# Mixer's context keys: the low word of each first key half made on VectorE from PSUM

## The chip, the cores and the metric

One core of one Trainium2 chip runs the whole program in one launch. The metric is the device time of one execution in microseconds; several runs are taken and their median is compared. One further execution is profiled.

## The reference

The program is a two-layer latent network on x (4 x 256 x 256) and a context (4 x 4096 x 256), all in float32. Each step is added to x and works on a layer-normed x:

```python
x = x + L0_xattn(_layernorm(x), ctx, ctx, mask, ...)    # 1 head of width 1024, masked
x = x + L0_attn(_layernorm(x), ...)                     # the mixer: a selective scan
x = x + L0_ffn(_layernorm(x), ...)                      # soft mixture of experts
x = x + L1_xattn(_layernorm(x), ctx, ctx, ...)          # 16 heads of width 16
x = x + L1_attn(_layernorm(x), ...)                     # causal attention
x = x + L1_ffn(_layernorm(x), ...)                      # quantised MLP
```

The change touches the second line, in which the kernel also prepares the fourth. The mixer is, cut short:

```python
xx, res = split(x @ in_w.T);  xx = silu(causal_conv4(xx) + conv_b)
delta, B, C = split(xx @ xproj_w.T);  delta = softplus(delta @ dt_w.T + dt_b)
state = exp(delta * A) * state + delta * B * xx      # over 256 tokens, 512 channels, 16 states
y = (sum over states of C * state + xx * D) * silu(res);  out = y @ out_w.T
```

and the part of the fourth line that does not depend on x is k = key @ Wk.T + bk and v = value @ Wv.T + bv, for all 4 x 4096 rows of the context.

## The kernel before

All six steps run one after the other, with a barrier of all engines behind each (`mixer` ends with one). The stage in question is `mixer`. While its scan runs, a second stream of work, called the context, computes k and v of the fourth step and stores them to DRAM. Products of the context are exact to about float32 by words: an operand is held as a high word, rounded to the format that TensorE multiplies in one pass, and a low word, the remainder; `products` (line 149) multiplies high by high, high by low and low by high.

**The mixer's scan.** 64 units: 2 halves of the tokens x 4 tiles of 128 channels (m) x 8 pairs of states (q); `mx_unit` gives them. For a unit i ScalarE makes two decays into PSUM (`prepare`, line 1115, instruction at 1123), GpSimd multiplies delta * u by B (`inputs`, 911, at 923), VectorE scans (`recur`, 1204, at 1208), multiplies by C (`outputs`, 1217), adds the two states of every second unit (`added`, 1222), and TensorE sums into a PSUM bank by a product with the identity (`total`, 987, at 998). Decays of unit i wait for the scan of unit i - 2. In the first tile of channels of each half (units 0 to 7 and 32 to 39) TensorE also spreads rows of B and C over all partitions (`spread`, 977, at 984) and ScalarE copies them out (1113). Every eight units come ScalarE's steps of softplus: Abs and Exp (`decline`, 1093 and 1095) in units 1, 9, 17 and so on, Ln with table loads (`logarithm`, 1099) in units 4, 12, 20 and so on, with VectorE's parts at 1178, 1180, 1186, 1188 and 1198, and VectorE's gate at 1230 and 1233.

**The context.** 32 chunks of 512 context rows, four steps each (`Steps`, line 614): first key half (128 of 256 output channels), second key half, first values, second values. A key half m of chunk i goes so. TensorE makes six products into one PSUM bank (`keys`, 677). ScalarE reads the bank, adds bk and writes the high word (`rounded` with n = 0, line 728). TensorE then adds to the same bank the product of the negated identity and that high word (`remainder`, 685, product at 687), so that the bank holds the difference. ScalarE reads it again with bk added and writes the low word (`rounded` with n = 1, same line). SyncE stores both (`store_keys`, 638, at 641). A values step is 12 products of 256 columns (`values`, 690) and two copies by ScalarE (738). SyncE fetches the next chunks (635).

**The order** is written out by hand. Every engine goes through its own list of units, and `mx_context(new, part)` (803) says how many context steps are done by the first place (part 0, ahead of the unit's decays on ScalarE and of its sums on TensorE) and by the second (part 1, behind them). Units 0 to 7 and 32 to 39 take one step each, in the second place; the others take two or three. The first step of a chunk i stands in these units: chunks 1, 2, 17, 18 in 0, 4, 32, 36 (second place), in which `CTX_ALONE` (581) puts the remainder right behind the keys; chunks 3, 5, 6, 9, 10, 12, 13, 16 in 8, 11, 13, 18, 20, 23, 25, 30, and 19, 23, 24, 25, 29, 30, 31 in 40, 47, 49, 51, 58, 60, 62 (first place); chunks 4, 7, 8, 11, 14, 15 in 9, 14, 16, 21, 26, 28, and 20, 21, 22, 26, 27, 28 in 41, 43, 45, 52, 54, 56 (second place). Chunk 0 is done ahead of the scan. On ScalarE and TensorE a step of one half is interleaved with the remainder of the other, as the `step` functions show.

**The banks.** Three PSUM banks (5, 6, 7) are handed round in the order of `MX_ORDER` among keys, values, step sizes and spreads; `free` (934) makes TensorE wait until the user three places earlier is through with the bank, and for keys that is when the semaphore kr of that half has reached 2n + 2 (`mx_taken`, 855):

```python
def mx_taken(s, cs, kind, n, part=0):
    if kind == "keys":
        return cs[2][part], 2 * n + 2
```

In units 8 to 31 and 40 to 63, where no spreads are made, second values of a chunk so follow its first key half in the same bank.

Of the kernel before, what the change touches and what calls it, by code (L numbers as in the profile page):

```python
# [6 lines left out]
F32 = mybir.dt.float32  # L7
# [665 lines left out]
def context_pe(k, t, sems, bank, free):  # L673
    s, kp, kr, ks = sems
    pe, PS = k.pe, k.PS

    def keys(i, m):
        if i == 0:
            pe.wait_ge(s.words, 5)
        free("keys", i, m)  # L680
        wait_chunk(pe, s, i)
        products(k, PS[:, bank("keys", i, m), :], [[t["wk2"][:, a, kd, m * P:(m + 1) * P] for a in range(2)] for kd in range(KD)],
                 [[t["words"][:, i % 2, a, kd, :] for a in range(2)] for kd in range(KD)]).then_inc(kp[m], 1)

    def remainder(i, m):
        pe.wait_ge(kr[m], 2 * i + 1)
        pe.matmul(PS[:, bank("keys", i, m), :], t["minus"][:], t["keys"][:, m, 0, :], start=False, stop=True,
                  skip_group_check=True).then_inc(kp[m], 1)

    def values(i, pair):  # L690
        free("values", i, pair)
        for j in range(2):
            at = (2 * pair + j) * P
            last = products(k, PS[:, bank("values", i, pair), j * D:(j + 1) * D],
                            [[t["words"][:, i % 2, a, kd, at:at + P] for a in range(2)] for kd in range(KD)],
                            [[t["wv2"][:, a, kd, :] for a in range(2)] for kd in range(KD)])
        last.then_inc(s.vp, 1)

    def step(n):
        i, sub = n // 4, n % 4  # L700
        if i in CTX_ALONE and sub < 2:
            keys(i, sub)
            remainder(i, sub)
        elif i in CTX_ALONE:
            values(i, sub - 2)
        elif sub == 0:
            keys(i, 0)
        elif sub == 1:
            keys(i, 1)
            remainder(i, 0)  # L710
        elif sub == 2:
            values(i, 0)
            remainder(i, 1)
        else:
            values(i, 1)

    return Steps(step)


def context_act(k, t, sems, bank):  # L720
# [1 line left out]
    act = k.act  # L722

    def rounded(i, m, n):
        act.wait_ge(kp[m], 2 * i + n + 1)
        if n == 0 and i:
            act.wait_ge(ks[m], 32 * i)
        act.activation(t["keys"][:, m, n, :], k.PS[:, bank("keys", i, m), :], ACT.Identity,  # L728
                       bias=t["bk"][:, m:m + 1]).then_inc(kr[m], 1)
# [12 lines left out]
    def step(n):  # L742
        i, sub = n // 4, n % 4
        if i in CTX_ALONE and sub < 2:
            rounded(i, sub, 0)
            rounded(i, sub, 1)
        elif i in CTX_ALONE:
            values(i, sub - 2)
        elif sub == 0:
            rounded(i, 0, 0)  # L750
        elif sub == 1:
            rounded(i, 1, 0)
            rounded(i, 0, 1)
        elif sub == 2:
            values(i, 0)
            rounded(i, 1, 1)
        else:
            values(i, 1)

    return Steps(step)  # L760

# [382 lines left out]

def mixer_dve(k, t, s, ct, cs):
    dve, PS, DT = k.dve, k.PS, MX_DT
    norm_dve(k, 1)
    yt_dve(k, 1)

    dve.wait_ge(s.small, 80)  # L1150
    for m in range(DT):
# [4 lines left out]
        for j in range(1, MX_TAPS):  # L1156
            dve.wait_ge(s.tap, MX_TAPS * m + j)
            dve.scalar_tensor_tensor(u, t["xpad"][:, m % 2, :, j:j + S], t["conv_w"][:, m, j:j + 1], u,
                                     ALU.mult, ALU.add).then_inc(s.tap, 1)

    for half in range(2):
        b, cols = mx_bank(16 + half), slice(half * BANK, (half + 1) * BANK)
# [72 lines left out]
    for i in range(MX_UNITS + MX_SUM):  # L1235
        if i < MX_UNITS:
            recur(i)
        if mx_chunk(i, 7):
            remainder(mx_chunk(i, 7))
        if mx_chunk(i, 4):  # L1240
# [5 lines left out]
            outputs(i - MX_MUL)  # L1246
        if 0 <= i - MX_ADD < MX_UNITS and mx_added(i - MX_ADD):
            added(i - MX_ADD)
    for tile in range(NT):
        dve.wait_ge(s.out, tile + 1)  # L1250
        dve.tensor_tensor(k.X[:, tile, :], k.X[:, tile, :], PS[:, tile % 2, 0:D], ALU.add).then_inc(s.x, 1)
# [1737 lines left out]
```

## Time and profile before

| | |
|---|---|
| median of 3 runs | 2008.87 us (2008.55 to 2012.26) |
| the profiled execution's own time | 2010.82 us |
| its span, first to last instruction | 2009.5 us |
| mean granted clock of TensorE | 0.945 |
| first keys of the context at | 355.2 us |
| first and last scan start at | 404.9 and 742.6 us |

The profiled execution's time is its span and what lies around it. In the tables of rows, times are microseconds from the span's start, unless marked ns. PE is TensorE, PEld its weight loads, DVE VectorE, ACT ScalarE, POOL GpSimd, SPq the queue of SyncE. A row of a group by line has line, engine and operation, output <- inputs with shapes, count, then busy us and mean ns of one, then the idle time of the engine just before them and what ended it. A row of the timeline has start, length, engine, line, operation and shapes; xN says that N such followed each other, and the bracket gives the idle time before. Matmuls overlap, so that the distance from one's start to the next one's is shorter than a matmul's own length.

### The profile page before, as it was taken

What the parts mean: (1) busy time and instruction counts of PE and PEld (TensorE: products, weight loads), DVE (VectorE), ACT (ScalarE), POOL (GpSimd) and SP (SyncE); (2) the same over time, 40 slices, a digit from 0 to 9 for tenths busy, and PEclk for the clock granted to TensorE, in tenths of its full rate; (3) what the DMA queues carried; (4) which work ended last, traced back from release to release, by engine and by line L of the source; (5) the groups of instructions that cost most, each with busy time, mean ns of one, the idle gap of its engine ahead of it and who ended that gap; (6) DMA issues with size and microseconds to landing.
All of it is one profiled execution on the core that took longest, in us unless ns stands there. A gap on an engine that the chain in (4) does not pass through costs nothing. (4 is left out here: it accounts for less than half of the span.)

```text
span 2009.5 us, 32823 instructions
## 1 busy us (share of the span) xinstructions
PE 1791.3 (89%) x12553; PEld 1223.2 (61%) x12553; DVE 1469.5 (73%) x1717; ACT 1202.4 (60%) x2131; POOL 368.3 (18%) x238
## 2 busy tenths in 40 slices
PE   7989998879988994999997899999999999998754
PEld 5877776447755663788877455555555555555524
DVE  7646552468888884566664699999999999994475
ACT  1332332577777753344443288888888888993363
POOL 4223301035444441122222000010010000000000
PEclk8999998989999997999999799999999999998977
DMA  9798852128855862121214945566657646510000
GB/s 360 275 322 313 314 198 90 53 79 307 283 211 192 289 242 87 49 90 64 70 38 74 164 120 117 102 112 119 119 109 123 115 103 112 102 28 10 0 1 21
DMA packets 171769, 280.20 MB, mean 139 GB/s; under 512 B 21422, under 2 KB 100430, under 8 KB 164446
## 3 DMA queue, kind: packets, MB, share of 16 engines
q1 hardware_dynamic: 169886, 277.61, 49.0%
q8 instruction: 102, 1.67, 0.4%
q10 hardware_dynamic: 1728, 0.49, 0.1%
q14 instruction: 53, 0.43, 0.1%
HBM read 187.46 MB, written 88.14 MB: 137 GB/s over the span
## 5 line engine op out<-in xcount | busy, mean ns | idle before, releaser
L2321 DVE TENSOR_REDUCE xn_peaks<-psum 128x2 f32<-128x1024 f32 x512 | 621.9, 1224 | 40.3 <-PE psum L2128 32.4
L2278 ACT ACTIVATE moe_mix_transposed<-psum 128x512 f32<-128x512 f32 x1024 | 552.8, 597 | 70.4 <-PE psum L2133 20.9
L2133 PE MATMUL psum<-xn_q_stack,xn_k_words 50*128 50x256 f32 x2048 | 376.2, 306 | 6.7 <-DVE xn_peaks L2321 4.7
L2128 PE MATMUL psum<-xn_k_words,xn_q_stack 50*128 50x512 f32 x1024 | 372.2, 452 | 5.6 <-DMA xn_q_stack<-q_rows 4.0
L2133 PEld LDWEIGHTS psum<-xn_q_stack,xn_k_words 50*128 50x128 f32 x2048 | 249.3, 186 | 208.1 <-ACT moe_mix_transposed L2278 186.8
L2165 PE MATMUL psum<-moe_mix_transposed,xn_v 128*32 128x256 f32 x4096 | 328.2, 392 | 2.0 <-issue 0.3
L923 POOL TENSOR_TENSOR mx_state<-mx_du,mx_b_all_channels 128x1024 f32<-128x1024 f32 x64 | 156.4, 2444 | 237.1 <-ACT mx_c_all_channels L1113 114.5
L2128 PEld LDWEIGHTS psum<-xn_k_words,xn_q_stack 50*128 50x128 f32 x1024 | 185.7, 186 | 14.9 <-issue 9.1
L1208 DVE TENSOR_TENSOR_SCAN mx_state<-psum,mx_state 128x1024 f32<-128x1024 f32 x64 | 146.2, 2284 | 57.9 <-ACT psum L1123 37.8
L321 PE MATMUL psum<-xw_ctx_natural,xw_weights_transposed 128*128 128x256 f32 x512 | 126.7, 394 | 14.0 <-DVE xw_weights_transposed L473 13.7
L2165 PEld LDWEIGHTS psum<-moe_mix_transposed,xn_v 128*32 128x32 f32 x4096 | 81.7, 108 | 73.6 <-issue 8.0
L728 ACT ACTIVATE ctx_k_words<-psum,ctx_bk 128x512 fp32r<-128x512 f32 x128 | 85.3, 688 | 50.8 <-PE psum L153 41.1
L153 PE MATMUL psum<-ctx_chunk_words,ctx_wk_words 128*128 128x512 f32 x384 | 109.3, 427 | 7.0 <-DMA ctx_chunk_words<-ctx_words 4.0
L153 PE MATMUL psum<-ctx_wv_words,ctx_chunk_words 128*128 128x256 f32 x768 | 115.1, 300 | 0.1
L321 PEld LDWEIGHTS psum<-xw_ctx_natural,xw_weights_transposed 128*128 128x128 f32 x512 | 96.4, 197 | 29.2 <-DVE xw_weights_transposed L473 17.1
L153 PEld LDWEIGHTS psum<-ctx_wv_words,ctx_chunk_words 128*128 128x128 f32 x768 | 101.4, 192 | 17.1 <-issue 13.2
L1974 POOL CAST xn_neg_words<-xn_neg_max 128x4 fp32r<-128x4 f32 x32 | 6.1, 190 | 549.2 <-DVE xn_neg_max L2328 549.2
L153 PE MATMUL psum<-moe_w_words,moe_hidden_words 128*128 128x256 f32 x768 | 101.8, 291 | 5.2 <-issue 5.2
L153 PE MATMUL psum<-xw_ctx_transposed_words,xw_q_folded_words 128*128 128x512 f32 x384 | 100.2, 417 | 3.6 <-DVE xw_scores L455 3.0
L153 PE MATMUL psum<-moe_slot_input_words,moe_w_words 128*128 128x512 f32 x384 | 93.8, 400 | 10.2 <-ACT moe_hidden L1548 8.6
L153 PEld LDWEIGHTS psum<-moe_w_words,moe_hidden_words 128*128 128x128 f32 x768 | 95.9, 192 | 8.9 <-issue 8.9
L998 PE MATMUL psum<-mx_state,identity 128*128 128x512 f32 x192 | 96.2, 619 | 2.5 <-DVE mx_state L1222 2.5
(330 smaller groups left out, 2647.2 us busy)
## 6 DMA issues: line engine op xcount, KB each, us to landing
xn_k_words<-k_words SPq DMA_DIRECT2D x384, 128.0 KB, 6.4
ctx_words<-xw_ctx_transposed_words SPq DMA_DIRECT2D x64, 512.0 KB, 7.1
ctx_chunk_words<-ctx_words SPq DMA_DIRECT2D x64, 512.0 KB, 5.4
k_words<-ctx_k_words SPq DMA_DIRECT2D x128, 256.0 KB, 2.5
v_all<-ctx_v SPq DMA_DIRECT2D x32, 544.0 KB, 3.2
xn_v<-v_all SPq DMA_DIRECT2D x32, 544.0 KB, 5.0
xw_mask<-in_mask_BxSxS_ik SPq DMA_DIRECT2D x8, 2048.0 KB, 7.9
xw_ctx_natural<-in_ctx SPq DMA_DIRECT2D x32, 512.0 KB, 6.6
```

Of the source, the lines that this page charges most:

```text
L153: last = k.pe.matmul(out, l, r, start=(n == 0), stop=(n == len(terms) - 1))
L321: last = pe.matmul(PS[:, 5, 0:D], t["ET"][:, c % 2, j, :], t["ctxN"][:, c, j, :], start=(c + j == 0), stop=(c == CH - 1 and j == JC - 1))
L728: act.activation(t["keys"][:, m, n, :], k.PS[:, bank("keys", i, m), :], ACT.Identity, bias=t["bk"][:, m:m + 1]).then_inc(kr[m], 1)
L923: pool.tensor_tensor(t["state"][:, i % MX_STATES, :, :], t["du"][:, m % 2, None, :].to_broadcast([P, MX_NQ, MX_HALF]), t["Bb"][:, q * MX_N ...
L998: last = pe.matmul(PS[:, MX_Y, :], k.ident[:], t["state"][:, i % MX_STATES, j, :], start=(q + j == 0), stop=(q == MX_NU - 1 and j == parts ...
L1208: dve.tensor_tensor_scan(flat, t["decay"][i % MX_DECAYS].rearrange("p n t -> p (n t)"), flat, 0.0, ALU.mult, ALU.add).then_inc(s.scan, 1)
L1974: pool.tensor_copy(t["neg_words"][:, :, :, XN_SHIFT], neg).then_inc(s.words, 1)
L2128: return pe.matmul(PS[:, 2 * (x % 2) + a, :], Q[narrow_rows(a), m // XN_PAIRS % 2, m % XN_PAIRS, q * P:(q + 1) * P], K[m % XN_KSLOTS][narr ...
L2133: return pe.matmul(PS[:, narrow_bank("exp", n, step, a), half * S:(half + 1) * S], K[n % XN_KSLOTS][narrow_rows(a), kt * P:(kt + 1) * P], ...
L2165: last = pe.matmul(PS[W * j:W * (j + 1), XN_ACC, 0:S], t["V"][:, n % 2, at:at + W], t["weights"][:, step % 4, a, half, :], start=(step == ...
L2278: act.activation(t["weights"][:, step % 4, a, :, :], bank.rearrange("p (t s) -> p t s", t=2), ACT.Exp, scale=XN_SCALE).then_inc(s.taken, 1)
L2321: dve.tensor_reduce(t["peaks"][:, m % 2, q, :, c], PS[:, 2 * (x % 2):2 * (x % 2) + 2, :], AX.X, ALU.max).then_inc(s.top_read, 1)
```

## The change

For the first key half (m = 0) of every chunk, TensorE's product with the negated identity and ScalarE's second rounding go. In their place VectorE reads the bank once: (bank + bk) - high word, written as the low word, one scalar_tensor_tensor of 128x512 per chunk. The second key half stays as it was. ScalarE's rounding of a first half now waits for kp[0] at i + 1, since TensorE increments it once per chunk. VectorE waits for that rounding (kr[0] at 2i + 1) and itself brings kr[0] to 2i + 2, for which the stores and the next user of the bank wait, as before. VectorE's context steps stand behind its convolution (chunk 0) and else behind the scan of each unit, up to the steps of both places of that unit.

```diff
--- before.py
+++ after.py
@@ -700,14 +700,14 @@
         i, sub = n // 4, n % 4
         if i in CTX_ALONE and sub < 2:
             keys(i, sub)
-            remainder(i, sub)
+            if sub:
+                remainder(i, sub)
         elif i in CTX_ALONE:
             values(i, sub - 2)
         elif sub == 0:
             keys(i, 0)
         elif sub == 1:
             keys(i, 1)
-            remainder(i, 0)
         elif sub == 2:
             values(i, 0)
             remainder(i, 1)
@@ -722,7 +722,7 @@
     act = k.act
 
     def rounded(i, m, n):
-        act.wait_ge(kp[m], 2 * i + n + 1)
+        act.wait_ge(kp[m], 2 * i + n + 1 if m else i + 1)
         if n == 0 and i:
             act.wait_ge(ks[m], 32 * i)
         act.activation(t["keys"][:, m, n, :], k.PS[:, bank("keys", i, m), :], ACT.Identity,
@@ -743,19 +743,37 @@
         i, sub = n // 4, n % 4
         if i in CTX_ALONE and sub < 2:
             rounded(i, sub, 0)
-            rounded(i, sub, 1)
+            if sub:
+                rounded(i, sub, 1)
         elif i in CTX_ALONE:
             values(i, sub - 2)
         elif sub == 0:
             rounded(i, 0, 0)
         elif sub == 1:
             rounded(i, 1, 0)
-            rounded(i, 0, 1)
         elif sub == 2:
             values(i, 0)
             rounded(i, 1, 1)
         else:
             values(i, 1)
+
+    return Steps(step)
+
+
+
+
+def context_dve(k, t, sems, bank):
+    s, kp, kr, ks = sems
+    dve = k.dve
+
+    def step(n):
+        i, sub = n // 4, n % 4
+        if sub == 0:
+            dve.wait_ge(kr[0], 2 * i + 1)
+            if i:
+                dve.wait_ge(ks[0], 32 * i)
+            dve.scalar_tensor_tensor(t["keys"][:, 0, 1, :], k.PS[:, bank("keys", i, 0), :], t["bk"][:, 0:1],
+                                     t["keys"][:, 0, 0, :].bitcast(F32), ALU.add, ALU.subtract).then_inc(kr[0], 1)
 
     return Steps(step)
 
@@ -1144,6 +1162,7 @@
 
 def mixer_dve(k, t, s, ct, cs):
     dve, PS, DT = k.dve, k.PS, MX_DT
+    ctx = context_dve(k, ct, cs, mx_bank_of)
     norm_dve(k, 1)
     yt_dve(k, 1)
 
@@ -1157,6 +1176,7 @@
             dve.wait_ge(s.tap, MX_TAPS * m + j)
             dve.scalar_tensor_tensor(u, t["xpad"][:, m % 2, :, j:j + S], t["conv_w"][:, m, j:j + 1], u,
                                      ALU.mult, ALU.add).then_inc(s.tap, 1)
+    ctx.upto(MX_EARLY)
 
     for half in range(2):
         b, cols = mx_bank(16 + half), slice(half * BANK, (half + 1) * BANK)
@@ -1235,6 +1255,7 @@
     for i in range(MX_UNITS + MX_SUM):
         if i < MX_UNITS:
             recur(i)
+            ctx.upto(mx_context(i, 1))
         if mx_chunk(i, 7):
             remainder(mx_chunk(i, 7))
         if mx_chunk(i, 4):
@@ -1246,6 +1267,7 @@
             outputs(i - MX_MUL)
         if 0 <= i - MX_ADD < MX_UNITS and mx_added(i - MX_ADD):
             added(i - MX_ADD)
+    ctx.upto(CTX_STEPS)
     for tile in range(NT):
         dve.wait_ge(s.out, tile + 1)
         dve.tensor_tensor(k.X[:, tile, :], k.X[:, tile, :], PS[:, tile % 2, 0:D], ALU.add).then_inc(s.x, 1)
```

## Rows read from the trace of the kernel before

**Rows 1.** The page: busy time, share of the span and instructions of each engine.

```profile
PE 1791.3 (89%) x12553; PEld 1223.2 (61%) x12553; DVE 1469.5 (73%) x1717; ACT 1202.4 (60%) x2131; POOL 368.3 (18%) x238
```

**Rows 2.** Windows of the mixer: length, busy per engine, granted clock, DMA share, GB/s.

```profile
456.48:584.43 127.95, 118.85 (x591) 89.18 (x590) 106.42 (x82) 95.30 (x177) 57.69 (x24) 0.99 0.82 291
632.24:745.00 112.76, 107.22 (x543) 80.95 (x541) 100.02 (x76) 83.71 (x157) 54.84 (x23) 1.00 0.80 288
```

**Rows 3.** Groups by line, units 0 to 63; columns as in the page.

```profile
L1208 DVE TENSOR_TENSOR_SCAN mx_state<-psum,mx_state 128x1024 f32<-128x1024 f32 x64 | 146.2, 2284 | 57.9 <-ACT psum L1123 37.8 <-POOL mx_state L923 20.1
L728 ACT ACTIVATE ctx_k_words<-psum,ctx_bk 128x512 fp32r<-128x512 f32 x124 | 82.6, 688 | 49.2 <-PE psum L153 39.6 <-PE psum L687 5.3 <-DMA k_words<-ctx_k_words 4.3
L687 PE MATMUL psum<-ctx_k_words,ctx_minus_identity 128*128 128x512 f32 x62 | 26.6, 430 | 22.9 <-ACT ctx_k_words L728 22.7
L1230 DVE SCALAR_TENSOR_TENSOR mx_u<-mx_u,mx_skip,psum 128x512 f32<-128x512 f32 x7 | 5.0, 719 | 0.0
```

**Rows 4.** Timeline around chunk 19: start, us, engine, line, idle before and its end.

```profile
632.22 0.40 PE L687 MATMUL psum<-ctx_k_words,ctx_minus_identity 128*128 128x512 f32 x1
632.24 2.28 DVE L1208 TENSOR_TENSOR_SCAN mx_state<-psum,mx_state 128x1024 f32<-128x1024 f32 x1
632.45 1.60 PE L153 MATMUL psum<-ctx_wv_words,ctx_chunk_words 128*128 128x256 f32 x12
...
634.09 0.65 ACT L738 COPY ctx_v<-psum 128x256 f32<-128x256 f32 x2 [0.43 <-PE psum L153]
634.44 1.51 DVE L1217 TENSOR_TENSOR mx_state<-mx_state,mx_c_all_channels 128x1024 f32<-128x1024 f32 x1
...
635.84 1.28 ACT L1123 ACTIVATE psum<-mx_delta,mx_a 128x510 f32<-128x510 f32 x2
...
637.15 2.29 DVE L1208 TENSOR_TENSOR_SCAN mx_state<-psum,mx_state 128x1024 f32<-128x1024 f32 x1 [1.21 <-ACT psum L1123]
```

**Rows 5.** Timeline: scans 13, 14, 20, 21, 51 and 52, and a copy of values.

```profile
483.54 2.28 DVE L1208 TENSOR_TENSOR_SCAN mx_state<-psum,mx_state 128x1024 f32<-128x1024 f32 x1
...
487.72 2.27 DVE L1208 TENSOR_TENSOR_SCAN mx_state<-psum,mx_state 128x1024 f32<-128x1024 f32 x1
...
519.77 2.29 DVE L1208 TENSOR_TENSOR_SCAN mx_state<-psum,mx_state 128x1024 f32<-128x1024 f32 x1 [2.82 <-ACT psum L1123]
...
525.15 2.29 DVE L1208 TENSOR_TENSOR_SCAN mx_state<-psum,mx_state 128x1024 f32<-128x1024 f32 x1
...
684.64 2.28 DVE L1208 TENSOR_TENSOR_SCAN mx_state<-psum,mx_state 128x1024 f32<-128x1024 f32 x1
...
687.26 0.65 ACT L738 COPY ctx_v<-psum 128x256 f32<-128x256 f32 x2 [0.43 <-PE psum L153]
...
692.50 2.29 DVE L1208 TENSOR_TENSOR_SCAN mx_state<-psum,mx_state 128x1024 f32<-128x1024 f32 x1 [2.48 <-ACT psum L1123]
```

**Rows 6.** Timeline: second values of chunks 6, 9 and 10, and scan 18.

```profile
481.94 1.59 PE L153 MATMUL psum<-ctx_wv_words,ctx_chunk_words 128*128 128x256 f32 x12
...
507.92 2.28 DVE L1208 TENSOR_TENSOR_SCAN mx_state<-psum,mx_state 128x1024 f32<-128x1024 f32 x1
...
509.14 1.99 PE L153 MATMUL psum<-ctx_wv_words,ctx_chunk_words 128*128 128x256 f32 x12
...
515.61 1.60 PE L153 MATMUL psum<-ctx_wv_words,ctx_chunk_words 128*128 128x256 f32 x12
```

**Rows 7.** Timeline: scan 32, chunk 17's second rounding and the spread behind it.

```profile
584.43 2.27 DVE L1208 TENSOR_TENSOR_SCAN mx_state<-psum,mx_state 128x1024 f32<-128x1024 f32 x1
584.47 0.69 ACT L728 ACTIVATE ctx_k_words<-psum,ctx_bk 128x512 fp32r<-128x512 f32 x1 [0.59 <-PE psum L687]
...
585.22 0.97 PE L984 MATMUL psum<-mx_dt_b_c_words,mx_selector 128*128 128x512 f32 x2 [0.32 <-ACT ctx_k_words L728]
```

**Rows 8.** Timeline behind TensorE's wait in unit 36, and the window of its clock.

```profile
607.87 0.79 PE L687 MATMUL psum<-ctx_k_words,ctx_minus_identity 128*128 128x512 f32 x1 [4.48 <-ACT ctx_k_words L728]
...
608.00:612.00 4.00, 4.00 (x7) 2.15 (x8) 3.93 (x5) 3.30 (x7) 0.58 (x1) 0.50 0.35 131
```

## The prediction

> **What bounds the kernel now.** The page first: TensorE is busy for 89% of the span, VectorE for 73%, ScalarE for 60% [rows 1]. That is an average over six stages, so the windows of the mixer come next [rows 2]. A barrier ends the mixer, so its length goes one to one into the time. In the two stretches in which VectorE scans units 8 to 31 and 40 to 63, TensorE is busy 118.85 of 127.95 us and 107.22 of 112.76, VectorE 106.42 and 100.02. Nothing else is near, and the granted clock is 0.99 and 1.00. So TensorE leads and VectorE stands close behind it. The groups by line say how they are tied [rows 3]: the scan waited 37.8 us in all for ScalarE's decays and 20.1 for GpSimd, and ScalarE's roundings waited 39.6 for TensorE's products. The chain is TensorE, ScalarE (strictly in order: roundings, copies of values, decays), scan. Work taken off TensorE or ScalarE should count here, unless something new holds TensorE.
>
> **What the change saves.** For each of 32 chunks, one product with the negated identity goes. It costs TensorE the distance from its start to the next product's, 632.22 to 632.45, so 0.23 us [rows 4]; 27 of the 32 lie in the two dense stretches (chunks 3 to 16 and 19 to 31): 27 x 0.23 = 6.2 us. The other five I count at nothing: chunk 0 runs ahead of the scans, where TensorE later waits for ScalarE's silu, and the four single-filed chunks are priced below. One rounding of 0.69 us goes from ScalarE [rows 3]. It is on the path only where the scan waits for the decays of the unit in which the rounding stood; by the order in the code and the waits in front of the scans that holds for some 7 chunks (in units 15, 17, 20, 27, 44, 55, 57), at 0.6 us each: 4.2 us. The waits of TensorE before the removed products are half of the 22.9 us [rows 3], but in the dense stretches they are few, and in the single-filed ones the next product waits for the same bank. Savings: 10.4 us.
>
> **What it adds on VectorE.** 32 instructions that read 128x512 from PSUM and write SBUF. The trace has no such form with this order of operands; the nearest is the gate's scalar_tensor_tensor with a PSUM operand, 0.72 us [rows 3]. The low end is 0.69, the mean of the ScalarE rounding that it replaces [rows 3], the high end the 1.51 us that a larger tensor_tensor took [rows 4], should GpSimd hold it up; I take 0.72. That is 23 us against 57.9 us in which the scan waits, so nearly all fits in. With chunks 3 to 16 VectorE comes to 106.4 + 10.1 of 128.0 us, with 19 to 31 to 100.0 + 9.4 of 112.8. Only near the end, where scans follow without a wait, do I let two of them through: 1.4 us.
>
> **What it moves: the bank.** This is the term that decides. PSUM has three banks for this work, taken in turn: first keys, second keys, first values, second values. In the dense stretches the second values product of a chunk takes the bank of its first keys. So far that was free when ScalarE's second rounding was done. Now it is free when VectorE's instruction is, and VectorE issues it behind the scan of the unit in whose steps the first keys stand. TensorE runs ahead of the scan by about a unit; where the first keys stand ahead of the decays of that unit, it arrives too early and is held. ScalarE then copies the values late, and where that copy stands in front of the next unit's decays, the next scan is late too.
>
> Chunk 19 shows the ring [rows 4]. Scan 40 starts at 632.24 and takes 2.28, the new instruction 0.72, values to their copy 634.09 - 632.45 = 1.64, and from the copy's start to the next scan (abs, exp and decays lie between) 637.15 - 634.09 = 3.06. Sum 7.70 us from scan to scan, where it was 4.91: 2.8 us more. Six chunks are of this kind: 3, 6, 10, 13, 19 and 25. Chunk 3 has abs and exp too: 2.8. Chunks 6, 10 and 13 have only the decays between, 0.55 for the copy and 1.31 to the scan [rows 4], ring 6.50; their pitches were 487.72 - 483.54 = 4.18 and 525.15 - 519.77 = 5.38 [rows 5], and 13 is taken as 10: 2.3 + 1.1 + 1.1. Chunk 25 has a logarithm between with its table loads, 692.50 - 687.26 = 5.24 [rows 5], ring 9.88 against 7.86: 2.0. Together 12.1 us.
>
> In nine more chunks (5, 9, 12, 16, 23, 24, 29, 30, 31) the copy stands behind the next decays, so there is a unit more of room, and only TensorE's lead is lost. Chunk 9: the bank comes free at 507.92 + 2.28 + 0.72 = 510.92, the values started at 509.14 [rows 6], so TensorE stands 1.8 us. Three others (5, 24, 30) are like it with less; as TensorE has little idle time to make it up, I take 4 x 1.2 = 5 us. In the other twelve the first keys stand behind the unit's decays, the scan is then half done when they come, and I count nothing. Chunk 10 holds TensorE worst, from 515.61 [rows 6] to 519.77 + 2.29 + 0.72 = 522.78 [rows 5], 7.2 us; it then has idle time behind it, and I let 2 us pass beyond the 1.1 above. Together 7.
>
> The keys of chunks 1, 2, 17 and 18 stand alone in their units, and three products later the same bank takes the next unit's spread of C or B. Chunk 17: the spread started at 585.22, behind ScalarE's second rounding of 584.47 [rows 7]; now the bank is free at 584.43 + 2.27 + 0.72 = 587.42, 2.2 us later, and GpSimd and the scan stand behind that spread. The other three have a scan that is about 1 us behind the old rounding: 5.2 us together.
>
> The stores to DRAM of chunk i's first keys start as much later; the next chunk's first rounding waits for them, some 7 us behind, by when TensorE is late as well. I count nothing more for that, nor for the fetches, which hang on values that are late anyway. The prologue's instruction sits where VectorE has nothing to do until the x projection, and is free.
>
> **Sum.** 12.1 + 7 + 5.2 + 1.4 - 10.4 = +15.3 us. On the profiled execution's 2010.82 us this gives 2026.1; the three runs shown have the median 2008.87, 1.95 below it, so the forecast is 2024.2 us.
>
> **The rivals.** *TensorE sets the pace and the ring closes by itself* (faster). If after a first hold or two TensorE stays so far behind the scan that the bank is free each time it comes, only the savings and the two late instructions remain: -10.4 + 1.4 = -9.0, time 1999.9. It decides once TensorE's lead at the second values is under scan plus instruction, 3.0 us. For it: TensorE leads the load, and in chunks 4, 7, 8, 14 and 15 the bank would have been free in time. Against it: in chunks 6 and 10 TensorE came 486.54 - 481.94 = 4.6 and 7.2 us too early [rows 5, 6], because ScalarE's table loads and VectorE's softplus held the scan and not TensorE; such leads come back every eight units. 20%.
>
> *Costs and savings cancel*: half of the bank's price, with all savings, gives +3, time 2012; and with less it is nothing to be measured. 10%.
>
> *The clock falls too* (slower still). Behind an idle time of 4.48 us the removed product took 0.79 us in place of 0.40, and the 4 us from 608 ran at 0.50 of the clock, the 1.2 GHz level [rows 8]. They gave 2 us of work, and the stretch behind still lost some. Four holds of over 2.5 us (6, 10, then 19 with 635.24 - 632.45 = 2.8 [rows 4], and 3 taken like it) would cost some 2.5 us each, +10 on the forecast: 2034. The Trainium skill, "TensorE: Matmul & The Clock Gate", Part 1, says that the throttled state is the default and activity releases it; by that rule each long hold costs this much again, and the trace agrees for that one wait. But in the dense stretches, short waits and all, the clock held 0.99 and 1.00 [rows 2], so I count it apart. 12%.
>
> *VectorE becomes the bound*: with 109.4 of 112.8 us in the last stretch, a small stretching of the new instruction against GpSimd would be seen whole; at 1.51 us each 32 x 0.8 = 25 us more, of which a third would show: 2033. 5%. The forecast itself has 53%.
>
> **Range and chances.** A difference of 0.2%, 4 us, is about what a measurement of this kernel can tell from none. Forecast bounds: if every hold passes whole (4 x 1.8, 6.1 for chunk 10, 4 x 2.2 for the single ones) and half the savings fail, +26; with the clock, +33, so 2042. Below, the first rival's 1999.9 is just left out, and most of its spread is held by 2001. Of the forecast's cases alone the range is 2012 to 2035. Slower by over 4 us: forecast, clock and VectorE, 0.70; within 0.10; faster 0.20.
>
> **What would show it.** Right: TensorE has new waits for VectorE's low word, in front of the second values products, long ones in chunks 3, 6, 10, 19, and in front of spreads; scans 9, 14, 41 and 52 are 2 to 3 us further behind the ones before; fewer ScalarE waits for the product. Wrong: if those waits are short or stand in few chunks and the pitches of the scans fall, the first rival holds; if TensorE's clock in the dense stretches falls under 0.97, the third; if the new instruction takes over 0.8 us, the fourth.

## The result and the profile after

The changed kernel takes 2035.82 us (median of seven runs, 2023.21 to 2046.86); the kernel before, run beside it, takes 2012.08 (seven runs, 2005.91 to 2024.28). The ratio is 1.0131, with a 95% interval of 1.0097 to 1.0166: slower by some 26 us by the ratio, 23.7 by the medians. The forecast was 15.3 us slower, 2024.2 us, with a range of 2001 to 2042. The sign and the mechanism hold; the size is too small. The profiled execution took 2042.8 us, 32.0 more than that of before and 7.0 above the median of its own kernel.

The page of the changed kernel, section 1 (before: [rows 1]):

```profile
PE 1794.8 (88%) x12521; PEld 1224.4 (60%) x12521; DVE 1483.0 (73%) x1749; ACT 1184.1 (58%) x2099; POOL 370.4 (18%) x238
```

32 products and 32 activations are gone and 32 instructions of VectorE have come. But TensorE's busy time rose by 3.5 us, although 32 products are missing: something makes the others longer. The windows, from scan 8 to scan 32 and from scan 40 to scan 63, show it, and so does the third line, the 2.97 us of one step of values (columns as in [rows 2]). The line by itself below them is the kernel before, from scan 40 to scan 63, since the second window of [rows 2] ends 2.4 us behind the start of scan 63:

```profile
454.36:597.95 143.59, 121.51 (x577) 91.25 (x577) 113.98 (x97) 88.42 (x166) 57.63 (x24) 0.93 0.73 260
649.67:767.59 117.92, 107.23 (x526) 80.67 (x526) 104.99 (x88) 76.12 (x143) 54.81 (x23) 0.97 0.76 266
652.65:655.62 2.97, 2.97 (x13) 2.97 (x14) 1.08 (x1) 0.00 (x0) 1.75 (x1) 0.52 0.74 277
```

```profile
632.24:742.59 110.35, 105.47 (x540) 80.52 (x539) 97.61 (x74) 83.06 (x155) 54.84 (x23) 1.00 0.81 287
```

The first stretch is 15.6 us longer than in [rows 2], the second 7.6 longer than before, and the granted clock fell from 0.99 and 1.00 to 0.93 and 0.97. In the small window it is 0.52, close to the 1.2 GHz level.

Groups by line, from 400 to 770 us (before: [rows 3]; the scan's line is now 1228, the new instruction 775, the decays 1141, the outputs 1237, GpSimd's inputs 941):

```profile
L1228 DVE TENSOR_TENSOR_SCAN mx_state<-psum,mx_state 128x1024 f32<-128x1024 f32 x64 | 146.2, 2285 | 73.3 <-ACT psum L1141 43.9 <-POOL mx_state L941 29.3
L153 PE MATMUL psum<-ctx_wv_words,ctx_chunk_words 128*128 128x256 f32 x744 | 116.0, 309 | 26.8 <-DVE ctx_k_words L775 26.6
L1002 PE MATMUL psum<-mx_dt_b_c_words,mx_selector 128*128 128x512 f32 x58 | 25.2, 496 | 18.5 <-DVE ctx_k_words L775 15.3 <-ACT ctx_v L738 2.0 <-ACT ctx_k_words L728 1.3
L775 DVE SCALAR_TENSOR_TENSOR ctx_k_words<-psum,ctx_bk,ctx_k_words 128x512 fp32r<-128x512 f32 x31 | 22.5, 725 | 2.0 <-ACT ctx_k_words L728 2.0
L687 PE MATMUL psum<-ctx_k_words,ctx_minus_identity 128*128 128x512 f32 x31 | 13.4, 433 | 7.9 <-ACT ctx_k_words L728 7.8
```

Read the right side first. The new instruction takes 725 ns, as forecast, and hardly waits (2.0 us in all). The waits it causes stand on TensorE: 26.6 us in front of values, 15.3 in front of spreads (and one of 4.4 in front of step sizes). The scan's own waits rose from 57.9 to 73.3 us, by 6.1 for ScalarE's decays and by 9.2 for GpSimd, whose inputs need the spreads.

Chunk 19 again, where [rows 4] show before. The timeline of the changed kernel:

```profile
649.67 2.28 DVE L1228 TENSOR_TENSOR_SCAN mx_state<-psum,mx_state 128x1024 f32<-128x1024 f32 x1
...
651.87 0.72 DVE L775 SCALAR_TENSOR_TENSOR ctx_k_words<-psum,ctx_bk,ctx_k_words 128x512 fp32r<-128x512 f32 x1
...
652.65 2.93 PE L153 MATMUL psum<-ctx_wv_words,ctx_chunk_words 128*128 128x256 f32 x12 [2.83 <-DVE ctx_k_words L775]
...
655.62 0.65 ACT L738 COPY ctx_v<-psum 128x256 f32<-128x256 f32 x2 [4.76 <-PE psum L153]
...
657.37 1.28 ACT L1141 ACTIVATE psum<-mx_delta,mx_a 128x510 f32<-128x510 f32 x2
...
658.69 2.29 DVE L1228 TENSOR_TENSOR_SCAN mx_state<-psum,mx_state 128x1024 f32<-128x1024 f32 x1 [4.96 <-ACT psum L1141]
```

This is the ring of the forecast: scan, new instruction, values, copy, decays, scan. The hold of TensorE is 2.83 us (forecast 2.8). From the scan to the values 2.98 us (forecast 3.00), from the copy to the next scan 3.07 (forecast 3.06). Only the middle link is off: values to copy 655.62 - 652.65 = 2.97 instead of 1.64. The ring is 9.02 us where 7.70 was forecast and 4.91 was before.

Scans of the two kernels, counted from scan 0, give a sum free of the other stages: scan 0 to scan 63 is 742.59 - 404.93 = 337.7 us before and 767.59 - 400.81 = 366.8 after, +29.1. The rest of the profiled 32.0 is -4.1 in front of scan 0 and +7.0 behind scan 63, most of it in stages that the change doesn't touch. All experiments below are read by this distance as well as by their times, since the times of one kernel spread by 20 us. The distance comes from one execution of each kernel; stretches with the same code differed by up to 1.3 us from trace to trace (117.92 us here and 116.65 in run 6, from scan 40 to scan 63).

### The profile page after: what moved, and what is told of

Its sections match the earlier page's. It is cut to its first block and busy times, and to the rows that moved or that the text cites. A ratio compares the mean times of both kernels' runs of the same rounds, so it can differ in the third digit from the quotient of the medians.

```text
span 2041.5 us, 32790 instructions
## 1 busy us (share of the span) xinstructions
PE 1794.8 (88%) x12521; PEld 1224.4 (60%) x12521; DVE 1483.0 (73%) x1749; ACT 1184.1 (58%) x2099; POOL 370.4 (18%) x238
## 5 line engine op out<-in xcount | busy, mean ns | idle before, releaser
L2155 PE MATMUL psum<-xn_q_stack,xn_k_words 50*128 50x256 f32 x2048 | 380.5, 309 | 9.6 <-ACT xn_q_whole L2274 4.3
L2150 PE MATMUL psum<-xn_k_words,xn_q_stack 50*128 50x512 f32 x1024 | 376.3, 456 | 5.6 <-DMA xn_q_stack<-q_rows 4.0
L1228 DVE TENSOR_TENSOR_SCAN mx_state<-psum,mx_state 128x1024 f32<-128x1024 f32 x64 | 146.2, 2285 | 73.3 <-ACT psum L1141 43.9
L153 PE MATMUL psum<-ctx_wv_words,ctx_chunk_words 128*128 128x256 f32 x768 | 120.0, 309 | 26.8 <-DVE ctx_k_words L775 26.6
L321 PE MATMUL psum<-xw_ctx_natural,xw_weights_transposed 128*128 128x256 f32 x512 | 122.9, 385 | 12.1 <-DVE xw_weights_transposed L473 11.8
L1016 PE MATMUL psum<-mx_state,identity 128*128 128x512 f32 x192 | 101.1, 646 | 4.1 <-DVE mx_state L1242 4.0
L728 ACT ACTIVATE ctx_k_words<-psum,ctx_bk 128x512 fp32r<-128x512 f32 x96 | 66.0, 690 | 48.4 <-PE psum L153 42.5
```

The source lines that it names most:

```text
L153: last = k.pe.matmul(out, l, r, start=(n == 0), stop=(n == len(terms) - 1))
L321: last = pe.matmul(PS[:, 5, 0:D], t["ET"][:, c % 2, j, :], t["ctxN"][:, c, j, :], start=(c + j == 0), stop=(c == CH - 1 and j == JC - 1))
L1016: last = pe.matmul(PS[:, MX_Y, :], k.ident[:], t["state"][:, i % MX_STATES, j, :], start=(q + j == 0), stop=(q == MX_NU - 1 and j == parts ...
L1228: dve.tensor_tensor_scan(flat, t["decay"][i % MX_DECAYS].rearrange("p n t -> p (n t)"), flat, 0.0, ALU.mult, ALU.add).then_inc(s.scan, 1)
L2150: return pe.matmul(PS[:, 2 * (x % 2) + a, :], Q[narrow_rows(a), m // XN_PAIRS % 2, m % XN_PAIRS, q * P:(q + 1) * P], K[m % XN_KSLOTS][narr ...
L2155: return pe.matmul(PS[:, narrow_bank("exp", n, step, a), half * S:(half + 1) * S], K[n % XN_KSLOTS][narrow_rows(a), kt * P:(kt + 1) * P], ...
```

## The experiments

Diffs are against the changed kernel. "Scans" is the distance from scan 0 to scan 63 less the 337.7 us of before. No version that computes the whole result beats the kernel before by a difference that came twice. The kernel before ran beside each group, with medians of 2008.96 (the first four), 2009.13 (the next four), 2010.11 (three) and 2006.73 us (the last).

**1. hold_only**: the kernel before, with the wait alone: the next user of the bank of a first key half also waits for the scan in whose unit the half stands. Nothing is saved and VectorE has no new instruction.

```diff
 # in free(); keys, rounding and product as before the change
+            last = MX_ORDER[MX_USE[use] - CTX_BANKS]
+            pe.wait_ge(*mx_taken(s, cs, *last))
+            if last[0] == "keys" and last[1] and last[2] == 0:
+                pe.wait_ge(s.scan, mx_unit_of(4 * last[1]) + 1)
```

> The kernel before, with one wait more: whoever takes the bank of a first key half (chunks 1 to 31) also waits for the scan behind which the change puts VectorE's instruction. All products and roundings stay, VectorE has nothing new. Theory (the late release of the bank is the cost): the distance from scan 0 to scan 63, 337.7 us before and 366.8 after, grows to 365 to 375, since the savings of 10.4 us are missing and only the 0.72 us behind each scan is gone; time 2036 to 2046. Rival (VectorE's 23 us of new work are the cost): under 345 us, time within 6 us of the kernel before.

Measured: 2033.44 us, ratio 1.0136 (1.0086 to 1.0186), scans +23.5. The hold alone, with every product still in place, costs nearly what the whole change costs (361.1 us from scan 0 to scan 63, where 365 to 375 were expected). Its timeline around chunk 19, and below it TensorE's values of chunks 6 and 10:

```profile
646.10 2.28 DVE L1216 TENSOR_TENSOR_SCAN mx_state<-psum,mx_state 128x1024 f32<-128x1024 f32 x1
...
648.53 1.67 PE L153 MATMUL psum<-ctx_wv_words,ctx_chunk_words 128*128 128x256 f32 x12 [2.09 <-DVE mx_state L1216]
...
653.30 2.29 DVE L1216 TENSOR_TENSOR_SCAN mx_state<-psum,mx_state 128x1024 f32<-128x1024 f32 x1 [3.52 <-ACT psum L1131]
...
484.13 2.85 PE L153 MATMUL psum<-ctx_wv_words,ctx_chunk_words 128*128 128x256 f32 x12 [4.10 <-DVE mx_state L1216]
...
525.95 2.90 PE L153 MATMUL psum<-ctx_wv_words,ctx_chunk_words 128*128 128x256 f32 x12 [6.43 <-DVE mx_state L1216]
```

This splits the middle link. Behind a hold of 2.09 us the same twelve products took 1.67 us, at a granted clock of 1.00; behind 4.10 and 6.43 they took 2.85 and 2.90, and in the changed kernel, behind 2.83, 2.93. With the clock up, chunk 19's ring is 653.30 - 646.10 = 7.20 us, by the forecast's links 2.28 + 1.7 + 3.06 = 7.0. So the ring is right for this chunk, and what was missing is the clock.

**2. saved_only**: the savings alone. The low word of first halves isn't computed (the high word is stored in its place too), so the bank is free after ScalarE's one rounding.

```diff
-        return cs[2][part], 2 * n + 2
+        return cs[2][part], 2 * n + 2 if part else n + 1
 # context_dve: the step does nothing; stores of m = 0 wait for i + 1
```

> The changed kernel without VectorE's instruction: the low word of the first key halves is left out (the high word is stored twice), the bank is free after ScalarE's rounding. It holds the savings alone. My sum has 10.4 us for them: scan 0 to scan 63 in 326 to 330 us, time about 10 us under before. Rival (TensorE and ScalarE did not bind, or each saving is taken up by the other's wait): 334 us or more, no difference in time.

Measured: 1996.39 us, ratio 0.993 (0.9905 to 0.9956), scans -15.5 (10.4 forecast). By scan 8 already -7.0, and -2.0 more from scan 32 to scan 40. These are the stretches of single-filed chunks, whose removed products and roundings the forecast counted at nothing. The two dense stretches give 6.6 together.

**3. dve_no_bank**: VectorE's instruction stays, but reads SBUF in place of the bank (the bias comes out as the low word), so the bank is free as in saved_only.

```diff
-t["keys"][:, 0, 1, :], k.PS[:, bank("keys", i, 0), :], t["bk"][:, 0:1],
+t["keys"][:, 0, 1, :], t["keys"][:, 0, 0, :].bitcast(F32), t["bk"][:, 0:1],
-        return cs[2][part], 2 * n + 2
+        return cs[2][part], 2 * n + 2 if part else 2 * n + 1
```

> The changed kernel, but VectorE's instruction reads the high word in SBUF in place of the bank, and the bank is free after ScalarE's rounding (so the low word of the first key halves is not computed: the bias is stored in its place). VectorE has the same 32 instructions in the same places, stores wait for them as in the changed kernel, TensorE does not. Theory: nearly free, scan 0 to scan 63 at most 4 us over the run with the savings alone, time 5 to 10 us under before. Rival (VectorE is the bound, or its wait for the rounding is the cost): 350 us or more.

Measured: 2013.79 us, ratio 1.0019 (0.9984 to 1.0055), scans +0.2: 28.9 less than the changed kernel, so the bank is the cost. But it is 15.7 over saved_only, where at most 4 was expected. Its groups by line (ScalarE's rounding, and the instruction):

```profile
L728 ACT ACTIVATE ctx_k_words<-psum,ctx_bk 128x512 fp32r<-128x512 f32 x93 | 64.1, 690 | 65.3 <-PE psum L153 36.3 <-DMA k_words<-ctx_k_words 26.4 <-PE psum L687 2.4
L775 DVE SCALAR_TENSOR_TENSOR ctx_k_words<-ctx_k_words,ctx_bk 128x512 fp32r<-128x512 f32 x31 | 28.0, 902 | 0.5 <-ACT ctx_k_words L728 0.5
```

ScalarE now waits 26.4 us for stores of the key halves (4.3 before, [rows 3]): both words are stored when the low one is done, and the next chunk's high word may not be written before. Run 7 takes that apart. And the form that reads SBUF alone takes 902 ns in the mean, not 725. This mean mixes two kinds, as the timeline shows, with GpSimd's instruction between them:

```profile
466.10 0.73 DVE L775 SCALAR_TENSOR_TENSOR ctx_k_words<-ctx_k_words,ctx_bk 128x512 fp32r<-128x512 f32 x1
...
504.81 2.39 POOL L941 TENSOR_TENSOR mx_state<-mx_du,mx_b_all_channels 128x1024 f32<-128x1024 f32 x1 [6.90 <-DVE mx_state L1242]
...
506.75 0.99 DVE L775 SCALAR_TENSOR_TENSOR ctx_k_words<-ctx_k_words,ctx_bk 128x512 fp32r<-128x512 f32 x1
```

The 13 that found no instruction of GpSimd under way took 0.72 to 0.75 us. The other 19 took 0.75 to 1.91, 17 of them the rest of GpSimd's instruction and 0.54 to 0.55 more: here 504.81 + 2.39 - 506.75 = 0.45, then 0.54.

**4. ahead**: the bank is read by VectorE in front of the scan of its unit where the first keys stand in the first place.

```diff
+            ctx.upto(mx_context(i, 0))      # ahead of the scan of unit i
```

> The changed kernel with VectorE's instruction ahead of the scan in the 15 chunks whose keys stand ahead of the unit's decays; in the other chunks it stays behind the scan. Theory: the holds of chunks 3, 5, 6, 9, 10, 12, 13, 16, 19, 23, 24, 25, 29, 30, 31 go, what stays are the single-filed chunks (about 6 us) and chunk 8 (about 1): scan 0 to scan 63 in 334 to 340 us, time within 6 us of before. Rival (VectorE in order now waits for ScalarE's rounding in front of its scan): 350 us or more.

Measured: 2015.5 us, ratio 1.0059 (1.0032 to 1.0086), scans +4.5. One line moved takes away 24.6 of the 29.1 us (342.2 us, where 334 to 340 were expected). By the times it takes away less, and the version is still slower than before: 0.59%, some 12 us, of which the scans show 4.5. Chunk 19, timeline:

```profile
632.00 0.75 DVE L775 SCALAR_TENSOR_TENSOR ctx_k_words<-psum,ctx_bk,ctx_k_words 128x512 fp32r<-128x512 f32 x1
...
632.67 2.28 DVE L1228 TENSOR_TENSOR_SCAN mx_state<-psum,mx_state 128x1024 f32<-128x1024 f32 x1
...
632.80 1.70 PE L153 MATMUL psum<-ctx_wv_words,ctx_chunk_words 128*128 128x256 f32 x12 [0.68 <-DVE ctx_k_words L775]
...
637.61 2.29 DVE L1228 TENSOR_TENSOR_SCAN mx_state<-psum,mx_state 128x1024 f32<-128x1024 f32 x1 [1.54 <-ACT psum L1141]
```

The hold is 0.68 us, the products take 1.70, and the pitch is 4.94 (4.91 before). Not every hold is gone: chunk 6 still has one of 2.08 us, with a pitch of 4.99 (4.18 before). The waits of TensorE for the instruction, the changed kernel first, in front of values (us in total, times, the longest):

```profile
PE psum L153 <- DVE ctx_k_words L775: 26.6, 12, 6.6
```

```profile
PE psum L153 <- DVE ctx_k_words L775: 7.4, 5, 3.0
PE psum L1002 <- DVE ctx_k_words L775: 15.4, 3, 6.6
```

The waits in front of spreads stay, 15.4 us: in the single-filed units the first keys stand in the second place, behind the scan.

**5. tight_old**: the six tight chunks the old way, 26 the new.

```diff
+CTX_LOW = [c for c in range(CTX_CHUNKS) if c not in (3, 6, 10, 13, 19, 25)]
 # remainder, second rounding and counts as before the change for chunks not in CTX_LOW
```

> The changed kernel, but chunks 3, 6, 10, 13, 19 and 25, whose values are copied ahead of the next unit's decays, keep TensorE's product and ScalarE's second rounding. VectorE still does the other 26. In the changed kernel the scans of units 9, 14, 21, 22, 26, 41 and 52 lost 21.5 us of its 29.1. Theory: they come back: scan 0 to scan 63 in 344 to 349 us (before 337.7, after 366.8), time 8 to 14 us over before. Rival (every late release costs alike, so these six are 6/31 of it): 359 to 363 us.

Measured: 2015.81 us, ratio 1.0036 (1.0011 to 1.006), scans +2.4. Six chunks of 32 carry 26.7 of the 29.1 us, more than the 21.5 that the expectation read from the pitches; the forecast gave them 12.1 (14.1 with chunk 10's lead). The other 26 together cost next to nothing, savings included.

**6. single_old**: the four single-filed chunks (1, 2, 17 and 18) the old way.

```diff
+CTX_LOW = [c for c in range(CTX_CHUNKS) if c not in CTX_ALONE]
```

> The changed kernel, but the single-filed chunks 1, 2, 17 and 18 keep the old way. In the changed kernel units 1 to 8 and 33 to 40 lost 2.0 and 3.9 us. Theory: they come back, scan 0 to scan 63 in 359 to 362 us. Rival: the run with the savings alone won 7.0 us in units 1 to 8, so those units may depend more on the removed product than on the late bank; then the old way wins nothing there and the distance stays at 365 or more.

Measured: 2034.97 us, ratio 1.0133 (1.0094 to 1.0173), scans +19.7, so by the scans these chunks cost 9.4 us net, 5.2 forecast. 8.0 of it lie in their own units (scans 0 to 8 and 32 to 40), 1.3 from scan 40 on, where the code is that of the changed kernel. The times don't confirm it: the ratio is that of the changed kernel, with four runs of this version.

**7. no_bank_split**: run 3, and the high word is stored by itself with its own semaphore, as soon as it is there; the low word later.

```diff
-        if sub in (1, 2):
-            store_keys(i, sub - 1)
+        if sub == 1:
+            store_word(i, 0, 0, s.kh)
+        if sub == 2:
+            store_word(i, 1, 0, ks[1])
+            store_word(i, 1, 1, ks[1])
+            store_word(i, 0, 1, ks[0])
```

> As dve_no_bank (VectorE's 32 instructions read SBUF, the bank is free after ScalarE's rounding, the bias is stored as low word), but SyncE stores the high word by itself as soon as it is rounded, and ScalarE's next rounding waits for that store and for VectorE's read, no longer for the store of VectorE's word. dve_no_bank took 337.8 us against 322.2 with the savings alone, and ScalarE waited 26.4 us for stores. Theory A (the late store closes a second ring): 322 to 330 us. Theory B (VectorE's time itself is the 15.6 us): 335 us or more.

Measured: 2003.99 us, ratio 0.9976 (0.9953 to 1.0), scans -7.8. So 8.0 of run 3's 15.7 us were the ring of stores, and 7.7 are left for VectorE's own time, at 0.91 us a piece. The group of ScalarE's rounding has no wait for a store left:

```profile
L733 ACT ACTIVATE ctx_k_words<-psum,ctx_bk 128x512 fp32r<-128x512 f32 x93 | 63.9, 689 | 50.6 <-PE psum L153 48.0 <-PE psum L690 2.4 <-DVE ctx_k_words L780 0.2
```

**8. best**: runs 4, 6 and the split stores together.

> A version put together from the parts: VectorE's instruction ahead of the scan where the keys stand ahead of the decays, the single-filed chunks by the old way, and the high word of the first half stored by itself, so that the next rounding does not wait for VectorE's store. From ahead (342.2 us from scan 0 to scan 63) less 5.9 for the single-filed chunks and 0 to 5 for the store: 331 to 337 us, time 0 to 6 us under before. Rival (VectorE in front of the scan, close to its bound, eats it): 340 us or more.

Measured: 2004.71 us, ratio 0.9983 (0.9962 to 1.0005), scans -0.9. Not told apart from before.

**9. all_ahead**: the instruction ahead of the scan in every unit of the single-filed kind, too, and split stores.

```diff
+            ctx.upto(mx_context(i, 0 if mx_unit(i)[1] else 1))      # ahead of the scan
```

> As best, but all chunks by VectorE, and in the single-filed chunks too its instruction stands ahead of the unit's scan, so that the bank is free before the third spread asks for it. Units 1 to 8 won 7.0 us with the savings alone and lost 2.0 in the changed kernel. Theory (where the instruction stands against the scan decides): scan 0 to scan 63 in 326 to 334 us, time 4 to 12 us under before. Rival (in these units the scan itself is late if VectorE waits for the rounding in front of it): 337 us or more.

Measured: 2006.03 us, ratio 0.9996 (0.9968 to 1.0024), scans -3.2. Scan 0 itself moves here; from the x projection to scan 63 it is 356.99 us, 360.47 before, 388.13 after. VectorE waits 5.8 us for ScalarE's high word, standing in front of a scan, 4.4 of them in front of scan 0, which had waited 3.8 before as well:

```profile
L780 DVE SCALAR_TENSOR_TENSOR ctx_k_words<-psum,ctx_bk,ctx_k_words 128x512 fp32r<-128x512 f32 x31 | 22.8, 735 | 6.1 <-ACT ctx_k_words L733 5.8 <-DMA k_words<-ctx_k_words 0.2
```

**10. tight_single_old**: the tight and the single-filed chunks the old way, the other 22 the new.

```diff
+CTX_LOW = [c for c in range(CTX_CHUNKS) if c not in (3, 6, 10, 13, 19, 25) + CTX_ALONE]
```

> The changed kernel, but the six tight chunks (3, 6, 10, 13, 19, 25) and the four single-filed ones (1, 2, 17, 18) by the old way, 22 chunks by VectorE behind the scan. tight_old took 340.0 us, single_old won 9.4 against the changed kernel. Theory: the parts add, 331 to 336 us, time within 5 us of before. Rival (they don't add, as the gain of single_old came from shorter holds behind it): 338 to 341.

Measured: 2004.05 us, ratio 0.9957 (0.9933 to 0.9982), scans -4.5: faster than both kernels by the interval. Its windows, scan 8 to scan 32 and scan 40 to scan 63:

```profile
446.66:570.55 123.89, 114.90 (x580) 86.22 (x578) 109.33 (x93) 89.57 (x167) 57.53 (x24) 1.00 0.84 298
618.60:729.37 110.77, 104.35 (x529) 78.41 (x528) 103.93 (x86) 76.67 (x144) 54.91 (x23) 1.00 0.80 284
```

The clock is back at 1.00. The first stretch is 4.1 us shorter than in [rows 2]; the second, 110.8 us to scan 63, is no shorter than the 110.4 of before. So the gain of the 22 chunks, where it is seen, lies in the first half.

**11. after_split**: the changed kernel with split stores.

> The changed kernel, in which SyncE stores the high word of the first half by itself as soon as it is rounded, and ScalarE's next rounding waits for that store and no longer for the store of VectorE's word. Without the bank's wait this was worth 8.0 us. Theory (with the bank held, TensorE is late anyway and the store does not bind): scan 0 to scan 63 in 362 to 368 us, against 366.8. Rival (the store's ring is in the 29.1 us as well): 360 us or less.

Measured: 2038.73 us, ratio 1.0146 (1.0092 to 1.02), scans +29.5. The stores of run 3 don't bind while the bank does.

**12. tight_single_split**: run 10 with split stores.

> As tight_single_old (22 chunks by VectorE behind the scan, ten by the old way), with the high word of the first half stored by itself, so that ScalarE's next rounding does not wait for the store of VectorE's word. Theory: the store binds where the bank does not hold TensorE, as in no_bank_split: 328 to 332 us from scan 0 to scan 63 (tight_single_old 333.1), time 1 to 5 us under tight_single_old. Rival (no store binds any more in this mix): 332.5 to 334.5 us, same time.

Measured: 2005.16 us, ratio 0.9999 (0.9978 to 1.002), scans -2.7. Splitting gives nothing more, and this near twin of run 10 doesn't repeat its gain against before. The medians of the two are 1.1 us apart, those of before beside them 3.4. A gain of some 0.1 to 0.2% is what the scans of both (-4.5 and -2.7) leave room for, the more so as 1.1 and 1.2 us of them lie in front of scan 8, where the code of the scans is that of before; it is not secured.

## Why the prediction came out as it did

**The mechanism is right.** The new waits are where they were forecast: 12 in front of values, 4 in front of spreads and step sizes. The hold alone gives +23.5 (run 1), reading the bank ahead of the scan takes 24.6 away (run 4), and freeing the bank while VectorE keeps its work takes 28.9 (run 3). The first rival, a ring that closes by itself, fell: each hold starts again, since TensorE regains its lead in between.

**The mis-sized term is that of the tight chunks**: "Together 12.1 us", with 2 us more for chunk 10. The pitches of the scans, before to after, give instead:

| chunk | scans | before | after | more | forecast | hold | values to copy |
|---|---|---|---|---|---|---|---|
| 3 | 8 to 9 | 4.59 | 8.84 | 4.25 | 2.8 | 3.15 | 2.81 |
| 6 | 13 to 14 | 4.18 | 7.83 | 3.65 | 2.3 | 4.14 | 2.97 |
| 10 | 20 to 22 | 9.61 | 14.71 | 5.10 | 3.1 | 6.64 | 2.96 |
| 13 | 25 to 26 | 4.99 | 6.59 | 1.60 | 1.1 | 1.85 | 1.72 |
| 19 | 40 to 41 | 4.91 | 9.02 | 4.11 | 2.8 | 2.83 | 2.97 |
| 25 | 51 to 52 | 7.86 | 10.71 | 2.85 | 2.0 | 2.29 | 2.50 |

The sum is 21.6 us against 14.1; in the traces of runs 6 and 11, where these chunks have the same code but for the stores, it is 20.1 and 19.4. Of the 7.5 us missing, the last column explains 6.1: each entry less the 1.64 us of [rows 4]. Two of these rows in the timeline of the changed kernel, with the windows of both products:

```profile
488.29 2.93 PE L153 MATMUL psum<-ctx_wv_words,ctx_chunk_words 128*128 128x256 f32 x12 [4.14 <-DVE ctx_k_words L775]
...
530.26 2.93 PE L153 MATMUL psum<-ctx_wv_words,ctx_chunk_words 128*128 128x256 f32 x12 [6.64 <-DVE ctx_k_words L775]
```

```profile
488.29:491.26 2.97, 2.97 (x13) 2.97 (x14) 1.68 (x2) 0.00 (x0) 1.12 (x1) 0.50 0.75 277
530.26:533.22 2.96, 2.96 (x13) 2.96 (x14) 2.89 (x4) 0.00 (x0) 0.00 (x0) 0.50 0.75 278
```

TensorE had stood still and then worked at 0.50, the 1.2 GHz level. So the third rival came true inside the forecast's own ring, in the chunks it named (3, 6, 10, 19) and partly in 25; in 13, held 1.85 us, it did not. It was not apart from the forecast, which had counted it as a case of its own: four of the six rings contain it. The length of the hold alone doesn't tell where it strikes, as two holds of other runs show, chunk 6 in run 4 and chunk 25 in run 6:

```profile
480.95 2.93 PE L153 MATMUL psum<-ctx_wv_words,ctx_chunk_words 128*128 128x256 f32 x12 [2.08 <-DVE ctx_k_words L775]
```

```profile
698.72 1.70 PE L153 MATMUL psum<-ctx_wv_words,ctx_chunk_words 128*128 128x256 f32 x12 [2.28 <-DVE ctx_k_words L784]
```

The shorter hold was followed by products at 0.50, the longer one by products at 1.00, and the hold of chunk 25 in the changed kernel, 2.29 us with the same code, by 0.63. So part of these 6.1 us is that one execution's. The rival's price was set at 2.5 us a hold; within the ring it is 1.2 to 1.3. What the low clock costs behind the copy (from 533.22 to 535.50 it is still 0.50) wasn't measured. Its criterion (clock under 0.97 in the dense stretches) is met in the first stretch, 0.93, and just not in the second, 0.97. The Trainium skill, "TensorE: Matmul & The Clock Gate", Part 1, says that the throttled state is the default and that activity releases it; the traces agree in so far as TensorE stood still for 2.8 us and more before each of these four. The forecast gave this case 12%, which was too little. Run 5's 26.7 us for the same six chunks is 5 more than the pitches show; what these 5 are, whether TensorE's lost lead further on, the clock behind the copy or their own savings, wasn't told apart.

**Where the sum was short.** Runs 5, 6 and 10 split the 29.1 us. The 22 chunks that are neither tight nor single-filed come to -4.5 (run 10); the forecast's terms without those ten chunks are 5 + 1.4 - 10.4 = -4.0, a little less negative without the tight chunks' own savings. The tight ones cost 24.2 us with the single-filed ones already the old way (run 6 less run 10) and 26.7 without, savings included, where the forecast has 14.1; the single-filed ones 6.9 and 9.4 in the same way, where it has 5.2. So the forecast was short in these ten chunks, mostly in the six.

**The bounds.** The forecast's upper bound is summed wrongly. With its own terms (4 x 1.8 for 5, 6.1 for 2, 4 x 2.2 for 5.2, half of the savings lost) the sum is 12.1 + 7.2 + 6.1 + 8.8 + 1.4 - 5.2 = +30.4, not +26, and with the clock's 10 us +40, so 2049 and not 2042. The measured time lies inside either.

**Single-filed chunks.** Forecast +5.2; net +6.9 to +9.4 by the scans (runs 6 and 10), and gross more, since the savings there are 8.9 (run 2). In chunk 17 the spread came 600.92 - 597.95 = 2.97 us behind the scan, by the forecast 2.99:

```profile
600.15 0.72 DVE L775 SCALAR_TENSOR_TENSOR ctx_k_words<-psum,ctx_bk,ctx_k_words 128x512 fp32r<-128x512 f32 x1
...
600.92 1.22 PE L1002 MATMUL psum<-mx_dt_b_c_words,mx_selector 128*128 128x512 f32 x2 [3.81 <-DVE ctx_k_words L775]
```

That place is right, at two products in 1.22 us where [rows 7] have 0.97. Wrong was the premise "the next product waits for the same bank" and with it "the other five I count at nothing": without the low word that bank is free earlier, and these stretches became 8.9 us shorter (run 2).

**Savings.** 10.4 forecast, 15.5 measured alone; in the dense stretches, where the forecast put all of it, 6.6. The seven roundings at 0.6 us and the 27 products at 0.23 don't both come through there.

**VectorE.** The duration is right, 725 ns for 0.72. Its price of 1.4 us wasn't measured by itself while the bank holds TensorE. With the bank free it is at most some 7.7 us (run 7, whose form takes 0.91 us where the change's takes 0.72). Likewise "I count nothing more" for the stores: true here (run 11: +29.5 for +29.1), but 8.0 us once the hold is gone.

**The terms don't add.** Hold alone +23.5, savings alone -15.5 and at most 7.7 for VectorE would give +16 at most; the change gives +29.1. In the units of the single-filed chunks the savings alone gave -8.9 and the hold alone +2.2, the change +5.9; in the dense stretches -6.6, +21.3 and +23.2. So with the hold in place the savings are not seen. That they lie in time in which TensorE and ScalarE wait anyway, so that the time is not there to be taken, fits the traces and has no run of its own. The new instruction itself lengthens each ring by its 0.72 us and with it the hold (chunk 19: 2.09 us at full clock without it, 2.83 at 0.52 with it).

## What to carry to other kernels

Before a PSUM reader is moved to another engine, write down the ring of that bank: who wants it next, how early, and behind what the new reader stands in its engine's order; then put the reader ahead of the long instruction, or leave the few tight places alone (here 6 of 32 carried 26.7 of 29.1 us). Neither made this kernel faster for certain; both only took back most of the loss. Price a hold of TensorE twice, once as a wait and once as the lower clock of the products behind it. And don't subtract savings that may fall into the time of that wait before a run with the wait has shown them.

## What the runs showed of the hardware

The twelve products of second values took 1.6 to 1.7 us behind waits for the bank of up to 1.72 us, at a granted clock of 1.00. Behind waits of 1.85 to 2.98 us they took anything from 1.67 to 2.93, in one case 1.70 and 2.46 behind the same wait of 2.3 us in two executions; behind waits of 3.15 to 6.64 they took 2.41 to 2.93, down to a clock of 0.50. So TensorE can change between its two levels behind waits of this kernel that are a single scan long, and not in the same way in every execution.

The second surprise is VectorE's. The scalar_tensor_tensor of 128x512 with one tensor from PSUM took 0.72 to 0.75 us in all 32 places of the changed kernel, in 16 of them beside an instruction of GpSimd that was under way. With its tensors from SBUF alone it took the same where GpSimd was idle, and the rest of GpSimd's instruction and some 0.54 us more where that had 0.28 us or more to go (run 3; run 7 shows the same).
